# Row sums of the layer norm on GpSimd, a sort half in PSUM, and 16 instead of 14 raw rows in a two-layer graph network

## The chip, the cores and the metric

The kernel runs on one NeuronCore of a Trainium2 chip. The metric is the device time of one execution in microseconds, as the median of several runs. Stages are read from one profiled execution. Engines are named TensorE (PE), VectorE (DVE), ScalarE (ACT), GpSimd (POOL) and SyncE (SP), the last of which only issues transfers here. A "gather" is an indirect DMA that GpSimd issues: it fetches one table row for each of 128 partitions.

## The reference

12,500 nodes with 256 features, 212,500 edges sorted by destination. The node features are normalized row by row, then two graph layers follow, and the input is added at the end.

```
h = relu(layernorm(x))
h = batchnorm(h, g0, b0)
for each of two layers:
    agg = segment_sum(h[src], dst)            # 212,500 edges
    h = relu(batchnorm((h + agg) @ W1 + b1))  # 256 x 256
    h = relu(h @ W2 + b2)
out = x + h
```

The layer norm of a row needs its sum, then the sum of the squares about the mean, then one scaled and shifted pass.

## The kernel before, in words

The nodes lie in 98 blocks of 128 rows (NB), 14 chunks (NCH) of 7 blocks (CH); all of them stay in the tile `acc`. The first seven chunks are the first half of the layer norm, the others the second (LB = 7). The edges are cut into 110 rows (NR) of 1932, one on each partition. `NPOS` and the copies of the table let one gather fetch several neighbouring source rows.

**Layer norm, ScalarE.** `ln_sums` (L977) makes seven row sums of a chunk as copies with an accumulated output, a small operation (L980) turns them into minus the mean, and `ln_squares` (L988) makes the sums of squares. A chunk's sums alternate with the squares of the chunk ahead. Roots are taken for each half (L995), then the raw copies (L1020) take the transposed edge lists out of PSUM into `src_raw` and `dst_raw`, and then `normalize` (L1001) writes the blocks. SyncE stores a chunk to the table `node_rows` as soon as it is normalized (`store_rows`, L565). The small arithmetic of the layer norm (`ln_variances`, `ln_rest`) is VectorE's and stands between the operations of its sort, at places that `LN_VAR_AT` and `LN_REST_AT` give and `beside_first` counts: place n is the n-th sort operation. Before, a pass of the first sort has two operations, each on 1024 elements.

**The sorts, VectorE.** For each of the 110 rows VectorE sorts 2048 keys twice in a bitonic network of 66 passes. The first 45 passes of the first sort (`in_sbuf`, L1296 and L1298) go from `keys` to `other` and back, both in SBUF. The last 21 passes and the whole second sort (`split_steps`, L1345) hold one half of the keys in SBUF and one in PSUM, so that each operation has one input of each, in four operations of 512 elements a pass. Between the sorts, and behind the second, VectorE builds the lists of source rows, lanes and codes. They are transposed on TensorE (`transpose_lists`), placed ahead of the raw group LISTS_AT, two groups before the end, and copied by ScalarE and VectorE.

**Raw rows.** The edges of the first RAWS = 14 rows are summed without the sorted lists: 16 gathers of 128 single edges a row (L679), 224 in all, each into one of RAW_SLOTS = 11 slots. Gather k waits until TensorE is done with gather k - 11. TensorE multiplies each by a one-hot matrix from ScalarE (`hot_of_raw`, L1041, L1045) at L779. This can begin once the table is stored, and lies beside the list building. SyncE puts the strided copies of the table beside it (L600), paced by `raw_done` up to COPIES_UNTIL. The sums are kept in `early` and merged by VectorE, MERGED_AT_ONCE for each row, into `acc` in the walk.

**The walk.** Rows 14 to 109 are then walked: 8 gathers a row (L697), 34 matmul instructions (L830), and VectorE adds the sums to the blocks (L1582). The gathers land in a ring of 38 places, two rows of edges. When the two blocks of a pair are complete, TensorE transposes them (L855) and multiplies by W1a (L872, L876); `pairs_late` says after which row, at most one pair a row, and none before row RAWS + 1. Layer 2 walks all 110 rows, in part twice.

**Order.** Each engine's queue is in program order, and waits stand in it. GpSimd's queue: constants, a cast and `node_steps` (L668), a wait for the stored table, 224 raw gathers, 768 gathers of walk 1, then layer 2. TensorE's queue ahead of the raw sums: the transposes of the raw lists (L728), 32 transposes of the edge lists into all eight banks (L735), a wait for the raw copies, two lane products, 98 products of the batch norm's mean (L746).

Of the kernel before, what the change touches and what calls it, by code (L numbers as in the profile page):

```python
# [14 lines left out]
P = 128  # L15
N = 12500
D = 256
# [8 lines left out]
CH = 7  # L26
NCH = NB // CH
LB = NCH // 2
# [14 lines left out]
LR = 1932  # L43
NR = (E + LR - 1) // LR
TAIL = E - (NR - 1) * LR
SORT = 2048
# [46 lines left out]
LN_VAR_AT = (18, 54)  # L93
LN_REST_AT = (30, 62)
# [3 lines left out]
RAWS = 14  # L98
RAW_TILES = RAWS * RAW
RAW_SLOTS = 11  # L100
# [8 lines left out]
FIRST_LANES_AT = 72  # L109
MERGED_AT_ONCE = 2  # L110
# [115 lines left out]
def build(nc, x, src, dst, g0, b0, W1a, b1a, g1, bt1, W1b, b1b, W2a, b2a, g2, bt2, W2b, b2b, out):  # L226
# [4 lines left out]
    with ctx:  # L231
# [6 lines left out]
        def sem(name):  # L238
            return ctx.enter_context(nc.semaphore(name))
# [101 lines left out]
        raw_ps = tr_ps + mm_ps + [set_ps, lane_ps] + agg_ps  # L341
# [34 lines left out]
        ln_summed = sem("ln_summed")  # L376
# [48 lines left out]


# [211 lines left out]
        def _(pool):  # L638
# [31 lines left out]

            pool.wait_ge(raw_lists_ready, 1)
# [48 lines left out]
        def _(pe):  # L720
# [10 lines left out]
            for of, banks in ((src_rows, raw_ps[0:4]), (dst_rows, raw_ps[4:8])):  # L731
                for j in range(RAW):
                    if banks[j // 4] is agg_ps[0]:
                        pe.wait_ge(raw_lists_ready, 1)
                    mm = pe.transpose(banks[j // 4][:, (j % 4) * P:(j % 4 + 1) * P], of[:, j * P:(j + 1) * P], ident[:, :])  # L735
            mm.then_inc(raw_transposed, 1)

            pe.wait_ge(raw_taken, 1)
# [8 lines left out]
            mm.then_inc(bn_summed, 1)  # L747

# [55 lines left out]
            for n in range(RAW_GROUPS):  # L804
                if n == LISTS_AT:
                    transpose_lists()
                sum_raw_group(n)
                if n == 0:
                    mean_columns()
                for q in pairs_beside(n):  # L810
                    transpose_pair(q)
# [155 lines left out]
        def _(act):  # L967
# [4 lines left out]
            def ln_sums(i, k):  # L972
                act.wait_ge(x_loaded[k], i * (32 if k == LB - 1 else 16) + 16)
                act.wait_ge(ln_squared, i * LB + max(k - 1, 0))
                first = (i * LB + k) * CH
                for b in range(first, first + CH):
                    ins = act.activation(unread[b % CH], block_of(b), ACT.Copy, accum_out=ln_sum[:, b:b + 1])  # L977
                ins.then_inc(ln_summed, 1)
                act.wait_ge(ln_summed, i * LB + k + 1)
                act.activation(ln_less[:, first:first + CH], ln_sum[:, first:first + CH], ACT.Copy, scale=-1.0 / D  # L980
                               ).then_inc(ln_centred, 1)

            def ln_squares(i, k):
                act.wait_ge(ln_centred, i * LB + k + 1)
                act.wait_ge(ln_squared, i * LB + k)
                first = (i * LB + k) * CH
                for b in range(first, first + CH):
                    ins = act.activation(unread[b % CH], block_of(b), ACT.Square, bias=ln_less[:, b:b + 1],  # L988
                                         accum_out=ln_square[:, b:b + 1])
                ins.then_inc(ln_squared, 1)  # L990
# [14 lines left out]
            def ln_stats_of(i, k0, k1):  # L1005
                for k in range(k0, k1):
                    if k < LB:
                        ln_sums(i, k)
                    if k:
                        ln_squares(i, k - 1)  # L1010
# [7 lines left out]
            for to, banks in ((src_raw, raw_ps[0:4]), (dst_raw, raw_ps[4:8])):  # L1018
                for h in range(0, RAW, 4):
                    ins = act.copy(to[:, h * NR:(h + 4) * NR].rearrange("p (j g) -> p j g", g=NR), bank_tiles(banks[h // 4]))  # L1020
            ins.then_inc(raw_taken, 1)
# [6 lines left out]
            normalize(1, 0, LB)  # L1028

# [96 lines left out]
        def _(dve):  # L1126
# [134 lines left out]
            setup(dve.memset(other[:, LR:SORT], REMOVED))  # L1261
# [22 lines left out]
            step(dve.scalar_tensor_tensor(other[:, 0:LR], self_edges, REMOVED, keys[:, 0:LR], ALU.mult, ALU.add))  # L1284

            def in_sbuf(of, to, runs, beside):

                half, n = 1, 0
                while half < runs:
                    by = half  # L1290
                    while by:
                        ins, outs = [t.rearrange("p (n k) -> p n k", k=2 * by) for t in (of, to)]
                        low = ins[:, :, 0:by]
                        high = ins[:, :, 2 * by - 1:by - 1:-1] if by == half else ins[:, :, by:2 * by]
                        after()
                        step(dve.tensor_tensor(outs[:, :, 0:by], low, high, ALU.min))  # L1296
                        beside(n)
                        step(dve.tensor_tensor(outs[:, :, by:2 * by], low, high, ALU.max))  # L1298
                        beside(n + 1)
                        of, to = to, of  # L1300
                        by //= 2
                        n += 2
                    half *= 2
                return of
# [496 lines left out]
```

## Time and profile before

| | |
|---|---|
| median of 3 runs | 2776.4 us (2771.52 to 2776.82) |
| the profiled execution | 2784.43 us, span 2782.6 us |
| TensorE busy | 2371.1 us (85%) |
| GpSimd busy | 1815.2 us (65%) |
| VectorE busy | 1739.1 us (62%) |
| ScalarE busy | 551.3 us (20%) |
| first gather / first gather of walk 1 / last gather of walk 1 | 161.06 / 469.07 / 1430.84 us |

Busy shares are means over stages with different limits. GpSimd's busy time counts 0.95 us for each gather; the 0.30 us between two of them is issue and not counted. Times of stages are from the start of the span.

### The profile page before, as it was taken

Reading aid. Unit: us, or ns where it says so; the run is one execution under the profiler, and the core shown is the slowest. Engines: PE = TensorE matmul, PEld = TensorE weight load, DVE = VectorE, ACT = ScalarE, POOL = GpSimd, SP = SyncE. Lnnn points to the kernel's source line nnn. Section 1 sums busy time; section 2 is a strip of 40 time slices with the busy share of each in tenths; the row PEclk is TensorE's granted clock in tenths of the full one; section 3 lists DMA queues with packets and bytes.
Section 4 is the critical chain, followed back from the end, with each engine's and each line's share of the span. In section 5 each row is a group of like instructions: output and inputs, shape, how many; then the busy total and the mean of one; then the engine's idle time right before and its main releaser. Section 6 shows DMA issues by size and latency. Waiting matters only on the chain.

```text
span 2782.6 us, 30723 instructions
## 1 busy us (share of the span) xinstructions
PE 2371.1 (85%) x10215; PEld 1827.6 (66%) x10215; DVE 1739.1 (62%) x3502; ACT 551.3 (20%) x1605; POOL 1815.2 (65%) x1894
## 2 busy tenths in 40 slices
PE   1466777999999999999979566699999999988979
PEld 1134433878877777777758444588888888776767
DVE  7999997755555555555548577555555555544459
ACT  8975544300000000000009311000000000000038
POOL 2058777777777777777740477677777777777720
PEclk8687766999999999999989899999999999999999
DMA  9387998888888888888848999888888888888868
GB/s 309 141 261 224 285 306 254 250 260 251 253 253 255 254 255 254 254 254 254 254 153 279 328 334 325 285 283 286 287 284 284 287 285 282 260 254 253 253 203 270
DMA packets 309364, 734.28 MB, mean 264 GB/s; under 512 B 41510, under 2 KB 183730, under 8 KB 309198
## 3 DMA queue, kind: packets, MB, share of 16 engines
q0 software_dynamic: 149184, 550.97, 63.2%
q1 hardware_dynamic: 160014, 181.25, 20.8%
q8 instruction: 86, 1.41, 0.2%
q14 instruction: 80, 0.66, 0.1%
HBM read 579.47 MB, written 152.59 MB: 263 GB/s over the span
## 4 chain that ended last, share of the span: by engine, by line
PE 51%; DMA 23%; POOL 8%; SPq 8%; ACT 5%; issue 4%; DVE 1%; DVEq 0%; ACTq 0%; POOLq 0%
PE agg_ps L830 35%; DMA rows<-node_rows,src_all 17%; SPq L617 7%; PE sort_ps L955 6%; PE sort_ps L872 5%; POOL rows L697 5%; DMA rows<-node_rows,raw_list 4%; PE sort_ps L876 2%; DMA raw_more<-node_rows,raw_list 2%; PE agg_ps L779 2%; ACT acc L1001 2%; POOL raw_more L679 2%; ACT lane_code L988 1%; ACT lane_code L977 1%; POOL rows L679 1%
## 5 line engine op out<-in xcount | busy, mean ns | idle before, releaser
L697 POOL DMA_INDIRECT rows<-node_rows,src_all x1648 | 1558.2, 946 | 642.6 <-issue 346.4
L830 PE MATMUL agg_ps<-rows,work 128*128 128x256 f32 (+1 forms) x7004 | 1630.3, 387 | 188.9 <-DMA rows<-node_rows,src_all 140.8
L830 PEld LDWEIGHTS agg_ps<-rows,work 128*128 128x128 f32 x7004 | 1297.7, 191 | 494.3 <-issue 133.9
L1582 DVE SCALAR_TENSOR_TENSOR acc<-agg_ps,in_first,acc 128x256 f32 (+1 forms) x286 | 138.7, 485 | 944.1 <-PE agg_ps L830 856.7
L1032 ACT ACTIVATE bn_root<-bn_var 128x2 f32<-128x2 f32 x3 | 0.6, 203 | 1860.2 <-DVE bn_var L1168 1860.2
L679 POOL DMA_INDIRECT rows<-node_rows,raw_list x124 | 129.2, 1042 | 174.8 <-DMA node_rows<-acc 137.3
L1534 DVE TENSOR_TENSOR work<-lane_code,lane_ps 128x1024 f32<-128x1024 f32 (+1 forms) x206 | 228.1, 1107 | 1.0 <-issue 1.0
L955 PE MATMUL sort_ps<-early,work 128*128 128x256 f32 x784 | 175.3, 388 | 22.1 <-ACT work L1117 11.5
L955 PEld LDWEIGHTS sort_ps<-early,work 128*128 128x128 f32 x784 | 140.2, 194 | 57.5 <-issue 25.6
L1543 DVE TENSOR_TENSOR work<-lane_code,lane_ps 128x640 f32<-128x640 f32 x206 | 167.7, 814 | 0.0
L1117 ACT ACTIVATE work<-acc,bn_shift,bn_scale 128x128 f32<-128x128 f32 x392 | 166.5, 485 | 3.3 <-DVE bn_shift L1179 2.8
L779 PE MATMUL agg_ps<-rows,lane_code 128*128 128x257 f32 (+1 forms) x248 | 109.8, 562 | 59.6 <-DMA rows<-node_rows,raw_list 56.6
L1582 DVE SCALAR_TENSOR_TENSOR acc<-agg_ps,in_second,acc 128x256 f32 (+1 forms) x286 | 136.1, 476 | 0.0
L1524 DVE SCALAR_TENSOR_TENSOR work<-lane_ps,lane_code,work 128x128 f32<-128x128 f32 x412 | 130.5, 342 | 0.0
L679 POOL DMA_INDIRECT raw_more<-node_rows,raw_list x100 | 110.6, 1106 | 30.5 <-issue 23.5
L779 PEld LDWEIGHTS agg_ps<-rows,lane_code 128*128 128x128 f32 (+1 forms) x248 | 55.2, 260 | 106.6 <-DMA rows<-node_rows,raw_list 79.3
L1106 ACT ACTIVATE acc<-acc,self_scale 128x257 f32<-128x257 f32 (+1 forms) x196 | 79.0, 495 | 193.4 <-DMA node_rows<-acc 176.8
L1538 DVE TENSOR_TENSOR work<-lane_code,lane_ps 128x384 f32<-128x384 f32 x206 | 112.7, 547 | 0.0
L1345 DVE TENSOR_TENSOR work<-work,sort_ps 128x512 f32<-128x512 f32 x168 | 108.0, 684 | 2.9
L779 PE MATMUL agg_ps<-raw_more,lane_code 128*128 128x257 f32 x200 | 81.3, 530 | 32.2 <-DMA raw_more<-node_rows,raw_list 31.9
L872 PE MATMUL sort_ps<-early,w_a 128*128 128x256 f32 x392 | 107.2, 396 | 1.3 <-DVE early L1611 1.3
L1345 DVE TENSOR_TENSOR sort_ps<-work,sort_ps 128x512 f32<-128x512 f32 x168 | 108.2, 690 | 0.0
(246 smaller groups left out, 1844.8 us busy)
## 6 DMA issues: line engine op xcount, KB each, us to landing
node_rows<-acc SPq DMA_DIRECT2D x113, 260.0 KB, 6.3
rows<-node_rows,src_all POOLq DMA_INDIRECT x1648, 4.4
node_rows<-acc SPq DMA_DIRECT2D x27, 910.0 KB, 4.3
node_rows<-acc SPq DMA_DIRECT2D x57, 390.0 KB, 5.4
node_rows<-acc SPq DMA_DIRECT2D x28, 650.0 KB, 8.6
node_rows<-acc SPq DMA_DIRECT2D x114, 130.0 KB, 4.6
acc<-in_x SPq DMA_DIRECT2D x13, 896.0 KB, 11.0
rows<-in_x SPq DMA_DIRECT2D x13, 896.0 KB, 7.3
```

The costliest lines, as they stand in the source:

```text
L617: sp.dma_start(to, of).then_inc(group_stored[i], 16)
L679: pool.indirect_dma_start(raw_rows[k % RAW_SLOTS], None, tables[0][0:NPOS, :], bass.IndirectOffsetOnAxis(raw_src[:, j * RAWS + g:j * RAWS ...
L697: pool.indirect_dma_start(tile_rows(k, 0, ROWS_OF[t] * DP), None, tables[layer][0:NPOS if t >= LAST_STRIDED else TABLE, :], bass.IndirectO ...
L779: pe.matmul(bank[:, 0:D + 1], raw_hots[n % RAW_HOTS][0:edges, (j - first) * P:(j - first + 1) * P], raw_rows[k % RAW_SLOTS][0:edges, 0:D + ...
L830: mm = pe.matmul(bank[:, 0:width], hot[:, unit * P:(unit + 1) * P], tile_rows(k, row, width), start=(start and n == 0), stop=(stop and n = ...
L872: mm = pe.matmul(to, w_a[layer][:, k, o * P:(o + 1) * P], sum_major[:, m % 2, k, :], start=(o == 0 and k == 0), stop=(last and k == KC - 1 ...
L955: mm = pe.matmul(mm_ps[b % 2][:, 0:D], act_major[:, b % CH, k, :], w_b[layer][:, k, :], start=(k == 0), stop=(k == KC - 1))
L1117: ins = act.activation(act_major[:, b % CH, k, :], half_block(b, k), ACT.Relu, bias=bn_shift[:, k:k + 1], scale=bn_scale[:, k:k + 1])
L1345: step(dve.tensor_tensor(place, low, high, op))
L1534: dve.tensor_tensor(hot[:, 0:2 * n * P].rearrange("p (j f) -> p j f", f=2 * P), codes[:, 0:n].unsqueeze(2).to_broadcast([P, n, 2 * P]), la ...
L1543: dve.tensor_tensor(hot[:, FIRST_AT[0] * P:(FIRST_AT[0] + m) * P].rearrange("p (j f) -> p j f", f=P), lanes[:, 0:m].unsqueeze(2).to_broadc ...
L1582: dve.scalar_tensor_tensor(to, sums, lanes[:, g:g + 1], to, ALU.mult, ALU.add).then_inc(sums_added, 1)
```

## The change

GpSimd gets the row sums of chunks 3 to 6 and 9 to 12, 56 of the 98 blocks, ahead of its wait for the stored table. It folds a chunk's seven blocks of 256 by adding halves: 128, 64, 32 columns, then the two chunks of a pair together, down to one. Each add waits for the one before it. ScalarE sums the other six chunks, in a new order, and makes all squares. The first sort goes through `split_steps` from its first pass. The raw copies need only two banks at a time, in turns with TensorE, and come after the normalizing. There are 16 raw rows in 9 slots, merged three at a time. The places between the sort's operations are doubled and shifted, as a pass now has four.

```diff
+SUMMED_BY_POOL = ((3, 4), (5, 6), (9, 10), (11, 12))
-LN_VAR_AT = (18, 54)
-LN_REST_AT = (30, 62)
-RAWS = 14
+LN_VAR_AT = (38, 68)
+LN_REST_AT = (50, 76)
+RAWS = 16
-RAW_SLOTS = 11
+RAW_SLOTS = 9
-FIRST_LANES_AT = 72
-MERGED_AT_ONCE = 2
+FIRST_LANES_AT = 96
+MERGED_AT_ONCE = 3
-        raw_ps = tr_ps + mm_ps + [set_ps, lane_ps] + agg_ps
+        raw_ps = [lane_ps, agg_ps[1]]
+        RAW_LISTS = [(of, first) for of in (src_rows, dst_rows) for first in range(0, RAW, 4)]
...
+            def add_halves(to, of, width):
+                nonlocal steps
+                if steps:
+                    pool.wait_ge(pool_step, steps)
+                pool.tensor_tensor(to, of[:, :, 0:width], of[:, :, width:2 * width], ALU.add).then_inc(pool_step, 1)
+                steps += 1
+
+            for i, chunks in enumerate(SUMMED_BY_POOL):
+                for n, c in enumerate(chunks):
+                    pool.wait_ge(x_loaded[c % LB], loaded_by(c))
+                    add_halves(half_sums, chunk_of(c), P)
+                    add_halves(half_sums[:, :, 0:64], half_sums, 64)
+                    add_halves(few_sums[:, n * CH:(n + 1) * CH, :], half_sums, 32)
+                for width in (16, 8, 4, 2):
+                    add_halves(few_sums[:, :, 0:width], few_sums, width)
+                add_halves(ln_sum[:, chunks[0] * CH:(chunks[1] + 1) * CH].unsqueeze(2), few_sums, 1)
+                pool.wait_ge(pool_step, steps)
+                pool.sem_inc(pool_summed, 1)
...
+            def transpose_raw(i):
+                if i >= len(raw_ps):
+                    pe.wait_ge(raw_taken, i - len(raw_ps) + 1)
+                of, first = RAW_LISTS[i]
+                for j in range(first, first + 4):
+                    mm = pe.transpose(raw_ps[i % 2][:, (j - first) * P:(j - first + 1) * P], of[:, j * P:(j + 1) * P], ident[:, :])
+                mm.then_inc(raw_transposed, 1)
+
+            pe.wait_ge(raw_lists_ready, 1)
+            for i in range(len(raw_ps)):
+                transpose_raw(i)
...
             mm.then_inc(bn_summed, 1)
+            for i in range(len(raw_ps), len(RAW_LISTS)):
+                transpose_raw(i)
...
+            def ln_pool_sums(i):
+                nonlocal centred
+                act.wait_ge(pool_summed, i + 1)
+                centre(SUMMED_BY_POOL[i][0], 2)
+                centred += 1
+                act.wait_ge(ln_centred, centred)
...
-            ln_stats_of(0, 0, LB + 1)
-            ln_stats_of(1, 0, 2)
+            for c in (0, 1, 2):
+                ln_sums(c)
+                ln_squares(c)
+            ln_sums(7)
+            ln_sums(8)
+            for i in (0, 1):
+                ln_pool_sums(i)
+                for c in SUMMED_BY_POOL[i]:
+                    ln_squares(c)
+            ln_squares(7)
+            ln_squares(8)
             ln_root_of(0)
-            ln_stats_of(1, 2, LB + 1)
-            act.wait_ge(raw_transposed, 1)
...
+            ln_sums(13)
+            ln_squares(13)
+            for i in (2, 3):
+                ln_pool_sums(i)
+                for c in SUMMED_BY_POOL[i]:
+                    ln_squares(c)
...
             normalize(1, 0, LB)
+            for i, (of, first) in enumerate(RAW_LISTS):
+                to = src_raw if of is src_rows else dst_raw
+                act.wait_ge(raw_transposed, i + 1)
+                act.copy(to[:, first * NR:(first + 4) * NR].rearrange("p (j g) -> p j g", g=NR), bank_tiles(raw_ps[i % 2])
+                         ).then_inc(raw_taken, 1)
...
-            runs = in_sbuf(other, keys, SORT // 4, beside_first)
-            dve.wait_ge(raw_taken, 1)
-            assert runs is keys
-            split_steps(SORT // 4, keys, other, keys)
+            split_steps(1, keys, other, keys, beside_first)
+            dve.wait_ge(raw_taken, len(RAW_LISTS))
```

## Rows read from the trace of the kernel before

**Rows 1.** Windows of GpSimd: stretch and length, busy (instructions), PE clock, DMA share, GB/s.

```profile
161.00:469.00 308.00, 239.78 (x224) 0.72 0.93 266
200.00:270.00 70.00, 58.69 (x38) 0.71 0.82 235
270.00:432.00 162.00, 122.58 (x130) 0.70 1.02 292
469.00:1432.00 963.00, 726.58 (x768) 0.99 0.82 254
```

**Rows 2.** The chain of waits behind the last normalized block: start, us, what.

```profile
155.89 4.27 DMA node_rows<-acc
```

**Rows 3.** Timeline of GpSimd, the first gather: start, us, operation [idle before it].

```profile
161.06 1.17 POOL L679 DMA_INDIRECT rows<-node_rows,raw_list  x1 [137.31 <-DMA node_rows<-acc]
```

**Rows 4.** Timeline of ScalarE in the layer norm.

```profile
25.53 0.42 ACT L977 ACTIVATE lane_code<-acc 128x256 f32<-128x256 f32 x1
...
28.58 0.49 ACT L988 ACTIVATE lane_code<-acc,bn_stats 128x256 f32<-128x256 f32 x1
...
32.21 0.42 ACT L977 ACTIVATE lane_code<-acc 128x256 f32<-128x256 f32 x1
...
65.55 1.28 ACT L995 ACT_TABLE_LOAD   x1
...
104.07 1.76 ACT L1020 CAST src_raw<-sort_ps 128x440 int16<-128x440 f32 x4
...
107.39 1.12 ACT L1001 ACTIVATE acc<-acc,bn_stats 128x256 f32<-128x256 f32 x2
```

**Rows 5.** The tile acc up to 110 us, by groups: ns min/median/max, first and last start.

```profile
L977 ACT ACTIVATE lane_code<-acc x84: 398/400/419, 6.1 to 95.9; 128x256 f32<-128x256 f32 x84
...
L552 SPq DMA_DIRECT2D acc<-in_x x6: 2495/2544/2782, 20.8 to 33.9; - x6
...
DMA to landing us min/median/max: 5.3/11.0/15.3
```

**Rows 6.** Timeline of VectorE: sort passes, and the wait for the raw sums.

```profile
37.38 1.23 DVE L1296 TENSOR_TENSOR work<-work 128x1024 f32<-128x1024 f32 x1
...
39.77 1.23 DVE L1296 TENSOR_TENSOR work<-work 128x1024 f32<-128x1024 f32 x1
...
268.50 1.28 DVE L1345 TENSOR_TENSOR work<-work,sort_ps 128x512 f32<-128x512 f32 x2
...
271.03 1.29 DVE L1345 TENSOR_TENSOR work<-work,sort_ps 128x512 f32<-128x512 f32 x2
...
472.76 0.95 DVE L1508 COPY lane_code<-set_ps 128x440 f32<-128x440 f32 x1 [8.62 <-PE agg_ps L779]
```

**Rows 7.** Timeline of GpSimd and VectorE in the setup.

```profile
10.60 0.23 POOL L664 TENSOR_SCALAR part_place<-part_col 128x1 f32<-128x1 f32 x1
...
19.50 4.25 POOL L668 TENSOR_TENSOR rows<-rows 128x1932 f32<-128x1932 f32 x1
...
20.42 5.36 DVE L1244 TENSOR_TENSOR rows<-work 128x1932 f32<-128x1932 int32 x1
...
25.81 2.29 DVE L1246 SCALAR_TENSOR_TENSOR rows<-work,rows 128x2048 f32<-128x2048 int32 x1
...
35.17 2.17 DVE L1284 SCALAR_TENSOR_TENSOR work<-rows,work 128x1932 f32<-128x1932 f32 x1
```

**Rows 8.** DMA issues: KB each, median us from issue to landing.

```profile
rows<-node_rows,raw_list POOLq DMA_INDIRECT x124, 6.7
```

**Rows 9.** The chain of waits in walk 1.

```profile
551.91 7.37 PE agg_ps L830 x34
...
563.26 7.37 PE agg_ps L830 x34
...
638.76 7.37 PE agg_ps L830 x34
...
657.52 7.37 PE agg_ps L830 x34
```

More of the change, by code:

```diff
@@ L423, in build, with loaded_by @@
         out_stored = sem("out_stored")
+        def loaded_by(c):
+            return 16 if c < LB else 48 if c == NCH - 1 else 32
         def block_of(b):
@@ L669, in _ @@
             assert done == POOL_SETUP
+            half_sums = rows[:, 4 * GIVEN + P:4 * GIVEN + P + CH * P].rearrange("p (b f) -> p b f", f=P)
+            few_sums = rows[:, 4 * GIVEN + P + CH * P:4 * GIVEN + P + CH * P + 2 * CH * 32].rearrange("p (b f) -> p b f", f=32)
+            steps = 0
+            def add_halves(to, of, width):
[15 more added lines that the diff above has]
+                pool.sem_inc(pool_summed, 1)
             pool.wait_ge(raw_lists_ready, 1)
@@ L809, in _ @@
                     mean_columns()
+                    pe.wait_ge(raw_taken, len(RAW_LISTS))
                 for q in pairs_beside(n):
@@ L970, in _ @@
             act.sem_inc(sum_taken, 2)
[L972 to L980, printed above, removed]
-                               ).then_inc(ln_centred, 1)
@@ L983, in ln_squares @@
[L983 to L990, printed above, removed]
+            passes = centred = 0
@@ new lines, in ln_pass, with centre @@
+            def ln_pass(c, step, done):
+                nonlocal passes
+                if passes:
+                    act.wait_ge(ln_passed, passes)
+                for b in range(c * CH, (c + 1) * CH):
+                    ins = step(b)
+                ins.then_inc(ln_passed, 1)
+                passes += 1
+                if done is not None:
+                    act.wait_ge(ln_passed, passes)
+                    act.sem_inc(done, 1)
+            def centre(c, chunks):
+                act.activation(ln_less[:, c * CH:(c + chunks) * CH], ln_sum[:, c * CH:(c + chunks) * CH], ACT.Copy, scale=-1.0 / D
+                               ).then_inc(ln_centred, 1)
@@ new lines, in ln_sums @@
+            def ln_sums(c):
+                nonlocal centred
+                act.wait_ge(x_loaded[c % LB], loaded_by(c))
+                ln_pass(c, lambda b: act.activation(unread[b % CH], block_of(b), ACT.Copy, accum_out=ln_sum[:, b:b + 1]), None)
+                act.wait_ge(ln_passed, passes)
+                centre(c, 1)
+                centred += 1
+                act.wait_ge(ln_centred, centred)
+            def ln_pool_sums(i):
+                nonlocal centred
+                act.wait_ge(pool_summed, i + 1)
+                centre(SUMMED_BY_POOL[i][0], 2)
+                centred += 1
+                act.wait_ge(ln_centred, centred)
@@ L1260, in _ @@
             dve.wait_ge(setup_done, done)
-            setup(dve.memset(other[:, LR:SORT], REMOVED))
+            setup(dve.memset(keys[:, LR:SORT], REMOVED))
             setup(dve.tensor_scalar(row_base[:, :], first_block[:, :], float(P), None, ALU.mult))
@@ L1283, in _, with split_steps @@
             dve.wait_ge(setup_done, done)
[L1284 to L1304, printed above, removed]
+            step(dve.scalar_tensor_tensor(keys[:, 0:LR], self_edges, REMOVED, keys[:, 0:LR], ALU.mult, ALU.add))
             def halves(sbuf, i):
                 return (sbuf[:, i * SORT // 2:(i + 1) * SORT // 2], sort_ps[:, i * SORT // 2:(i + 1) * SORT // 2])
-            def split_steps(half, of, sbuf, to):
-                turn = 0
+            def split_steps(half, of, sbuf, to, beside=None):
+                turn = n = 0
                 while half < SORT:
```

27 lines of the change are left out of this document (9 added, 18 removed).

## Prediction

> **What bounds the kernel now.** I read the windows of GpSimd first, then the chain of waits and the timeline at the ends of each stage. From its first gather to the end of the first walk GpSimd never rests: 224 raw gathers in 308.0 us, then 768 walk gathers in 963 us, 1.25 us each [rows 1, 3]. In the walk that pace holds to within 3 us (768 x 1.25 = 960), so there a row of edges costs 8 gathers, 10.0 us of GpSimd. In the raw stage 224 x 1.25 = 280, so 28 us are stretch; it lies almost wholly where VectorE builds lists (38 gathers in 70 us; at 1.25 they take 47.5). Beside the second sort there is none: 130 gathers in 162 us, 1.246 each [rows 1]. Vector's chain is second: it is out of work 8.62 us before the raw sums let it go on, at 464.1 us [rows 6]. Ahead of all that stands ScalarE: the last normalized block leaves at 155.89, its store lands 4.3 us later, and the first gather, after 137.31 us of waiting for that store, goes at 161.06 [rows 2, 3]. So two quantities decide: when the table is stored, and how many gathers GpSimd has to issue after it.
>
> **Part 1: row sums on GpSimd.** For ScalarE a chunk's sum pass is 28.58 - 25.53 = 3.05 us and its square pass 32.21 - 28.58 = 3.63 [rows 4]. Eight sum passes go (24.4 us), and the raw copies, 107.39 - 104.07 = 3.3 us, move behind the normalizing. That is 27.7 us at best, but the new order waits. ScalarE starts at 6.1 [rows 5], so chunks 0 to 2, both passes, end at 6.1 + 3 x 6.7 = 26.2. Chunk 7 is next; its load is issued at 20.8, and a load takes 11.0 us in the median: 31.8, up to 36.1 with the longest [rows 5]. Sums of 7 and 8 end at 38.0.
>
> GpSimd's price: its subtraction of 1932 elements took 4.25 us, 2.2 ns an element, and its one-element operation 0.23 [rows 7]. A pair of chunks is 2 x (896 + 448 + 224) + 434 = 3570 output elements in 11 instructions: 7.85 + 11 x 0.31 (0.23 and a gap of 0.08) = 11.3 us. Starting at 23.75, when the subtraction ends, pair 0 is done at 35.1 if nothing disturbs it.
>
> It is disturbed. Vector's comparison of 1932 elements began under that subtraction, took 5.36 us, and ended 2.03 us behind GpSimd's end, about what such a comparison needs alone (2.17 for the same length): it had stood still until GpSimd was through [rows 7]. The new adds begin exactly when Vector has its setup operations with two SBUF inputs to do (2.29, 2.17 and two more of that size, [rows 7]) and the first sort pass, whose two inputs are both in SBUF still. If each waits for one add (2.0, 1.0 or 0.5 us) and each add for one of them, Vector loses 5 to 10 us and pair 0 moves to about 45. I take 7; the ends are 0 (no alternation) and 10. In the Trainium skill, GPSIMD Engine Reference, sections "Specifications" and "Key points", the shared SBUF interface is contended by Vector instructions in a two-port mode or with two SBUF inputs. By it the setup collides, as I took from the row, and a sort pass with one input in PSUM doesn't; the 130 unstretched gathers of [rows 1] agree with the second half, and if the rule failed there the adds would collide all through the sort (rival 4).
>
> ScalarE's schedule from there: squares of 3 and 4 (7.3) to 52.3; pair 1 at 45 + 11.3 = 56.3, squares to 63.6; of 7 and 8 to 70.9. The root waits for Vector's variance at place 38 of the sort, 9.5 passes of 2.53 and 1.3 of list work behind 37.38, or 62.7, plus 7: covered. Root and table load 1.5, chunk 13 6.7, four square passes 14.8: 93.9, against 104.07. Without any collision the same steps give 38.0, 45.3, 53.7, 61.0, wait to 62.7, then 85.7. Normalizing takes 155.89 - 107.39 = 48.5, store and first gather 5.2 [rows 2 to 4]. First gather: 93.9 + 53.7 = 147.6, which is **13.5 us earlier**; 21.7 without collision, 11.5 with the full 10 us.
>
> **Part 2: the sort half in PSUM.** A pass costs 39.77 - 37.38 = 2.39 in SBUF and 271.03 - 268.50 = 2.53 mixed [rows 6]; 45 passes: +6 us on Vector. With 7 of collision and some 3 of waiting at place 68 (variance of the second half, due at 83 + 7, where the squares end at 93.9) its chain ends at 464.1 + 16 = 480. It is hidden by the raw stage, whose last lists are wanted at tile 248, near 490. Cost nothing; with that cover gone, what exceeds 10 us. The raw copies behind the normalizing (3.3 us and six turns with TensorE, about 10 us) lie beside the first gathers' latency; TensorE has nothing from them for the first 10 us today either. Up to 2 us.
>
> **Part 3: 16 raw rows in 9 slots.** 32 more raw gathers: +40.0 us. 16 fewer walk gathers: -20.0. The first gathers of the walk don't wait for anything else, so this is paid in full: +20.0. The 28 us of stretch stay, since both list builds still fall into the raw stage. With 11 slots a gather may be 13.75 us old before it stops GpSimd; with 9, 11.25. It lands after 6.7 in the median [rows 8], and a matmul follows. I take 1 us, the range 0 to 5.
>
> In the walk TensorE is slower than GpSimd where a pair is finished in each row (563.26 - 551.91 = 11.35 us a row) and faster afterwards (657.52 - 638.76 = 18.8 for two) [rows 9]. Today the pairs due early end at rows 15 to 25; by the planner's formula they will end at 17 to 29, thirteen in a row, while the walk starts two light rows nearer. The lead grows 1.35 us a row, and today's 3 us over 960 show the ring already full. Three more such rows: +4 us (0 to 6). MERGED_AT_ONCE 3 gives Vector one more merge a row, under that 11.35; nothing.
>
> **Sum.** -13.5 + 40.0 - 20.0 + 1 + 4 = **+11.5 us**. The profiled execution took 2784.4 (span 2782.6), 8.0 above the median shown; it would become 2795.9, and the median 2776.4 becomes **2787.9**. What a measurement of this kernel can tell from no change is about 0.2%, 5.5 us.
>
> **Rivals.**
> 1. No collision in the setup: the add and Vector's operations overlap, the gather starts at 139.4. -21.7 + 40 - 20 + 1 + 4 = +3.3, 2780, within 0.2%. For it: I read the collision from a single overlap. Against it: the 5.36 us row. Chance 0.22.
> 2. Faster: ScalarE never waits, neither for chunk 7 nor for GpSimd or the variance. Then the full 27.7 us, and with TensorE's extra rows also absorbed, -27.7 + 20 = -7.7, 2768.7. It decides from a first gather before 135.5 (20 + 5.5 below 161.06). For it: only 3 passes and 11 squares are left at 26.2, 51 us. Against it: chunk 7 can hardly land before 31. Chance 0.12.
> 3. GpSimd's adds are dearer, on narrow pieces of 1 to 16 elements above all. If a pair takes 15 us, pair 3 is done at 24 + 10 + 60 = 94, its squares at 101.3, the first gather goes at 155: -6 + 25 = +19. At 17 us it goes at 163, no earlier than now: +2 + 25 = +27, 2803. It decides from 13.2 us a pair (34 + 4 x 13.2 + 7.3 = 93.9 again). Against it: nothing in the rows but the price per element. Chance 0.10.
> 4. The mixed passes collide with the adds too: 44 adds at half a Vector operation of 0.63 us each is 14 us more on both engines, the first gather goes at about 155, +19, 2796. Against it: the second sort beside the gathers. Chance 0.04.
> The forecast itself has 0.52; its own range is +4 to +18.
>
> **Numbers.** Slower by over 0.2%: 0.52 less a little for its lower edge, with 3 and 4: 0.64. Within: 0.24. Faster: 0.12. Range: from no collision and no stalls (-21.7 + 20 = -1.7, a little below) to the full collision with all stalls (-11.5 + 20 + 6 + 5 = +19.5) and part of rival 3: **2773 to 2800**.
>
> **What would show it.** First raw gather at 147.6 (139 or 155: rivals 1, 4); the Vector setup and first pass ending near 47 instead of 40; pairs of adds of 11.3 us; ScalarE's stops at chunk 7, at pair 0 and pair 1; 256 raw gathers in about 349 us; 752 walk gathers in 946; first walk gather near 496, last one 11 us later than now; Vector waiting for raw sums, not the reverse. I am wrong if the start is before 136, if the raw stage stretches less than 28 us, or if GpSimd stops for lists or slots.

## The result, and the profile after

The changed kernel takes **2788.4 us** (median of 5 runs, 2786.2 to 2790.3) where the kernel before takes 2775.3 (5 runs, 2771.5 to 2776.8): a ratio of 1.0049 [1.0034, 1.0064], 13 us slower. The forecast was 2787.9 and slower.

Each stage is read from its first and last gather. The kernel before stands in the table twice, since a second profiled execution of it was taken with the experiments (`before_again`). Before, the raw copies lie ahead of the normalizing and take 3.3 of the 107.4 us.

| us from the start | before | before, again | after | forecast of after |
|---|---|---|---|---|
| normalizing begins | 107.4 | 107.8 | 97.3 | 93.9 |
| first gather | 161.1 | 161.5 | 150.9 | 147.6 |
| raw stage, its length | 308.0 | 306.6 | 350.9 | 349 |
| first gather of walk 1 | 469.1 | 469.6 | 501.8 | 496 |
| walk 1, its length | 961.8 | 961.1 | 945.8 | 946 |
| last gather of walk 1 | 1430.8 | 1430.6 | 1447.6 | |
| span | 2782.6 | 2770.4 | 2785.4 | |

Windows of GpSimd in the changed kernel, as in [rows 1]:

```profile
151.00:502.00 351.00, 271.43 (x257) 0.72 0.85 246
215.00:290.00 75.00, 62.42 (x42) 0.76 0.69 197
290.00:450.00 160.00, 119.82 (x127) 0.67 0.96 280
502.00:1448.00 946.00, 711.79 (x752) 0.99 0.82 253
```

The pace is that of before: 1.25 us a gather in the walk and beside the second sort (127 in 160 us), and a visible stretch only where lists are built (42 in 75 us, which at 1.25 take 52.5). So what moved is the start, 10.2 us earlier, and the number of gathers, 32 more before the walk and 16 fewer in it. The store's landing and the first gather, from the chain of waits and the timeline of GpSimd [rows 2, 3]:

```profile
145.70 4.28 DMA node_rows<-acc
```

```profile
150.88 1.19 POOL L710 DMA_INDIRECT rows<-node_rows,raw_list  x1 [71.67 <-DMA node_rows<-acc]
```

GpSimd's 137.3 us of waiting for the store have become 71.7: the adds take 55 us of time that it had to spare (23.9 to 79.2), and the store lands 10 us earlier. Their timeline (start, us, operation):

```profile
19.67 4.25 POOL L676 TENSOR_TENSOR rows<-rows 128x1932 f32<-128x1932 f32 x1
23.88 4.00 POOL L687 TENSOR_TENSOR rows<-acc 128x896 f32<-128x896 f32 x1
27.96 4.59 POOL L687 TENSOR_TENSOR rows<-rows 128x448 f32<-128x448 f32 x2
...
36.59 7.40 POOL L687 TENSOR_TENSOR rows<-rows 128x448 f32<-128x448 f32 x6
44.07 1.01 POOL L687 TENSOR_TENSOR bn_stats<-rows 128x14 f32<-128x14 f32 x1
...
58.02 2.10 POOL L687 TENSOR_TENSOR rows<-acc 128x896 f32<-128x896 f32 x1 [0.24 <-POOL bn_stats L687]
60.21 1.88 POOL L687 TENSOR_TENSOR rows<-rows 128x448 f32<-128x448 f32 x2
...
64.40 3.81 POOL L687 TENSOR_TENSOR rows<-rows 128x448 f32<-128x448 f32 x6
```

The same add of 896 elements takes 4.00 us at 23.88 and 2.10 at 58.02; the six narrow ones 7.40 and then 3.81. VectorE, at the same time:

```profile
20.58 5.36 DVE L1308 TENSOR_TENSOR rows<-work 128x1932 f32<-128x1932 int32 x1
25.98 4.05 DVE L1310 SCALAR_TENSOR_TENSOR rows<-work,rows 128x2048 f32<-128x2048 int32 x1
...
34.49 4.04 DVE L1316 SCALAR_TENSOR_TENSOR rows<-rows 128x1932 f32<-128x1932 f32 x1
...
45.93 4.89 DVE L1389 TENSOR_TENSOR sort_ps<-work 128x512 f32<-128x512 f32 x2
50.86 1.29 DVE L1389 TENSOR_TENSOR work<-work,sort_ps 128x512 f32<-128x512 f32 x2
```

The operation that took 2.29 us in [rows 7] takes 4.05, and the second sort pass starts at 50.86 where it started at 39.77 [rows 6]. From there on the passes have one input in PSUM, and neither they (2.53 us each) nor the adds (2.10) are slowed; some small operations of VectorE between the passes still are (late_adds, below). What waited for what between 16 and 150 us (us in total, times, longest):

```profile
ACT bn_stats L1026 <- POOLq L700: 11.9, 2, 6.7
ACT lane_code L1032 <- DMA acc<-in_x: 5.6, 1, 5.6
DVE bn_stats L1252 <- ACTq L1023: 2.4, 1, 2.4
ACT bn_stats L1052 <- DVE bn_stats L1252: 1.0, 1, 1.0
```

Of the 27.7 us that ScalarE was relieved of, 18.5 went to its own waits: 5.6 for chunk 7, 11.9 for the first two pairs of sums, 1.0 for the variance. Before, it waited 3.2 us in the same stretch, for a load, so the waits have grown by 15.3. At the other end, around 500 us, VectorE's timeline shows that its lists now have time to spare:

```profile
494.20 0.17 DVE L1540 TENSOR_SCALAR_CACHE_REDUCE check_sum<-lane_ps 128x12 f32<-128x12 f32 x1 [15.07 <-PE lane_ps L825]
...
505.51 0.95 DVE L1553 COPY lane_code<-set_ps 128x440 f32<-128x440 f32 x1 [8.68 <-PE agg_ps L817]
```

The wait for the raw sums, 8.7 us, is as it was [rows 6]; the one for TensorE ahead of it has grown from 2.6 to 15.1. In walk 1 the chain of waits shows TensorE at 11.35 us a row as in [rows 9], from the first of these lines to the last in ten steps:

```profile
562.52 7.37 PE agg_ps L869 x34
573.87 7.37 PE agg_ps L869 x34
...
676.00 7.37 PE agg_ps L869 x34
```

### The profile page after: what moved, and what is told of

Its sections match the earlier page's. It is cut to its first block, busy times and chain, and to the rows that moved or that the text cites. A ratio compares the mean times of both kernels' runs of the same rounds, so it can differ in the third digit from the quotient of the medians.

```text
span 2785.4 us, 30795 instructions
## 1 busy us (share of the span) xinstructions
PE 2375.7 (85%) x10211; PEld 1826.7 (66%) x10211; DVE 1750.0 (63%) x3580; ACT 544.2 (20%) x1531; POOL 1885.3 (68%) x1954
## 4 chain that ended last, share of the span: by engine, by line
PE 49%; DMA 23%; POOL 10%; SPq 7%; issue 5%; ACT 4%; DVE 3%; DVEq 0%; ACTq 0%; POOLq 0%
PE agg_ps L869 31%; DMA rows<-node_rows,src_all 16%; POOL rows L728 7%; SPq L625 7%; PE sort_ps L994 6%; PE sort_ps L911 5%; DMA rows<-node_rows,raw_list 4%; PE agg_ps L817 3%; PE sort_ps L915 2%; DMA raw_more<-node_rows,raw_list 2%; ACT acc L1058 2%; POOL rows L710 1%; ACT acc L1170 1%; POOL raw_more L710 1%; PE sort_ps L894 1%
## 5 line engine op out<-in xcount | busy, mean ns | idle before, releaser
L869 PEld LDWEIGHTS agg_ps<-rows,work 128*128 128x128 f32 x6936 | 1282.2, 191 | 481.5 <-issue 120.0
L710 POOL DMA_INDIRECT rows<-node_rows,raw_list x172 | 183.5, 1067 | 123.8 <-DMA node_rows<-acc 71.7
L817 PE MATMUL agg_ps<-rows,lane_code 128*128 128x257 f32 (+1 forms) x344 | 139.8, 528 | 75.0 <-DMA rows<-node_rows,raw_list 72.2
L994 PE MATMUL sort_ps<-early,work 128*128 128x256 f32 x784 | 174.2, 386 | 19.6 <-ACT work L1181 11.3
L1389 DVE TENSOR_TENSOR work<-work,sort_ps 128x512 f32<-128x512 f32 x258 | 166.2, 683 | 4.3
L1389 DVE TENSOR_TENSOR sort_ps<-work,sort_ps 128x512 f32<-128x512 f32 x258 | 166.3, 688 | 0.0
L817 PEld LDWEIGHTS agg_ps<-rows,lane_code 128*128 128x128 f32 (+1 forms) x344 | 75.0, 250 | 130.7 <-DMA rows<-node_rows,raw_list 96.5
L911 PE MATMUL sort_ps<-early,w_a 128*128 128x256 f32 x392 | 107.8, 398 | 1.5 <-DVE early L1656 1.5
L817 PE MATMUL agg_ps<-raw_more,lane_code 128*128 128x257 f32 (+1 forms) x168 | 74.4, 569 | 38.0 <-DMA raw_more<-node_rows,raw_list 37.6
L710 POOL DMA_INDIRECT raw_more<-node_rows,raw_list x84 | 87.9, 1046 | 27.2 <-issue 18.3
```

What stands on the lines that cost most here:

```text
L710: pool.indirect_dma_start(raw_rows[k % RAW_SLOTS], None, tables[0][0:NPOS, :], bass.IndirectOffsetOnAxis(raw_src[:, j * RAWS + g:j * RAWS ...
L817: pe.matmul(bank[:, 0:D + 1], raw_hots[n % RAW_HOTS][0:edges, (j - first) * P:(j - first + 1) * P], raw_rows[k % RAW_SLOTS][0:edges, 0:D + ...
L869: mm = pe.matmul(bank[:, 0:width], hot[:, unit * P:(unit + 1) * P], tile_rows(k, row, width), start=(start and n == 0), stop=(stop and n = ...
L911: mm = pe.matmul(to, w_a[layer][:, k, o * P:(o + 1) * P], sum_major[:, m % 2, k, :], start=(o == 0 and k == 0), stop=(last and k == KC - 1 ...
L994: mm = pe.matmul(mm_ps[b % 2][:, 0:D], act_major[:, b % CH, k, :], w_b[layer][:, k, :], start=(k == 0), stop=(k == KC - 1))
L1389: step(dve.tensor_tensor(place, low, high, op))
```

## The experiments

All profiles are read as above. "Lists" is when VectorE has written the last list word, "gap" the idle time of GpSimd just before its first walk gather (0.3 where it doesn't wait). "Before beside it" is the median of the kernel before in the same session; sessions differ, so kernels are compared by their ratios.

| kernel | first gather | lists | gap | first walk gather | last of walk 1 | time | before beside it | ratio |
|---|---|---|---|---|---|---|---|---|
| before, again | 161.5 | 459.4 | 0.3 | 469.6 | 1430.6 | | | |
| after | 150.9 | 479.1 | 0.3 | 501.8 | 1447.6 | 2788.4 | 2775.3 | 1.0049 [1.0034, 1.0064] |
| rows_alone | 161.3 | 459.5 | 0.3 | 509.6 | 1454.9 | 2796.6 | 2774.6 | 1.0076 [1.0060, 1.0093] |
| sums_14 | 150.3 | 478.6 | 30.6 | 483.9 | 1446.6 | 2788.6 | 2774.6 | 1.0050 [1.0034, 1.0067] |
| rows_15 | 151.0 | 480.2 | 8.6 | 485.6 | 1439.0 | 2780.8 | 2774.6 | 1.0020 [1.0011, 1.0030] |
| late_adds | 154.5 | 483.3 | 0.3 | 502.2 | 1446.9 | 2788.1 | 2774.6 | 1.0052 [1.0035, 1.0069] |
| adds_sbuf | 167.1 | 491.5 | 0.3 | 520.4 | 1466.2 | 2812.1 | 2777.6 | 1.0117 [1.0100, 1.0135] |
| copies_behind | 157.7 | 458.6 | 0.3 | 467.5 | 1429.8 | 2774.3 | 2777.6 | 0.9988 [0.9979, 0.9997] |
| psum_sort | 160.0 | 466.8 | 4.2 | 472.1 | 1433.9 | 2782.8 | 2777.6 | 1.0018 [1.0009, 1.0027] |
| three_pairs | 141.4 | 469.5 | 5.7 | 475.0 | 1428.5 | 2775.3 | 2777.6 | 0.9994 [0.9985, 1.0003] |
| mixed_15 | 141.1 | 465.4 | 0.3 | 473.0 | 1425.7 | 2765.6 | 2772.2 | 0.9974 [0.9964, 0.9984] |

### rows_alone: the 16 rows without the rest

The kernel before, with the counts of the change alone.

```diff
-RAWS = 14
+RAWS = 16
-RAW_SLOTS = 11
+RAW_SLOTS = 9
-MERGED_AT_ONCE = 2
+MERGED_AT_ONCE = 3
```

> The kernel before with 16 raw rows in 9 slots, merged three at a time, and nothing else of the change. My theory (GpSimd issues a gather each 1.25 us without rest, so 32 raw gathers more and 16 walk gathers fewer cost 20 us, and the ring in the walk some 4 to 8 more): first gather unchanged at 161, first walk gather 40 to 44 us later, last gather of walk 1 at 1451 to 1459, total 2775 + 20 to 28 = 2795 to 2803. Rival (the walk is TensorE's, a row there is worth 9.4 to 11.4 us of TensorE, so two rows fewer pay for the raw gathers in part): last walk gather at most 5 to 12 us later, total 2780 to 2787.

It took 2796.6 us, ratio 1.0076. The walk begins 40.0 us later than in the second look at before (509.6 to 469.6) and ends 24.3 later. This is the 40 - 20 + 4 of the forecast: from its first to its last gather walk 1 has 751 steps, 938.8 us at 1.25, and takes 6.5 more; the 767 steps of before (958.8) took 3.0 and 2.3 more. The raw stage is 28.3 us over its 320, and was 28.0 over its 280 before with 11 slots: the 9 slots cost nothing.

### sums_14: the changed kernel with 14 rows

```diff
-RAWS = 16
+RAWS = 14
-RAW_SLOTS = 9
+RAW_SLOTS = 11
-MERGED_AT_ONCE = 3
+MERGED_AT_ONCE = 2
```

> The changed kernel with 14 raw rows in 11 slots, merged two at a time: only the row sums on GpSimd and the sort half in PSUM are left of the change. My theory: first gather at 150.9, raw gathers end at 150.9 + 309.5 = 460, but VectorE's list chain ends only at 479 (20 us later than before, by collision, mixed passes and its wait for the variance), so GpSimd waits some 20 to 25 us for the lists and the walk starts at about 485; last walk gather about 1447, total 2785 to 2792, no better than 16 rows. Rival (the two extra raw rows are the whole loss): the walk starts at 460, total 2765 to 2768, faster than before by 0.3%.

It took 2788.6, the same as after. GpSimd's timeline at the end of the raw stage:

```profile
452.36 0.94 POOL L710 DMA_INDIRECT rows<-node_rows,raw_list  x1 [0.30 <-issue]
483.85 0.94 POOL L728 DMA_INDIRECT rows<-node_rows,src_all  x1 [30.55 <-issue]
```

GpSimd is through with its raw rows at 453 and stands still for 30.6 us, because VectorE's lists, 19.2 us later than before (478.6 to 459.4), aren't there. So the two extra rows of the change are filler for a hole that its other parts make: with 14 rows the lists set the start of the walk, with 16 the gathers do, and they cost 14 and 13 us.

### rows_15: one row between the two

```diff
-RAWS = 16
+RAWS = 15
-RAW_SLOTS = 9
+RAW_SLOTS = 10
```

> The changed kernel with 15 raw rows in 10 slots. My theory: 150.9 + 300 + 31 = 482, the lists are ready at about 484, so both chains end together: walk starts at about 485, 760 gathers in 955, last walk gather 1441, total 2780 to 2784. Rival (rows cost nothing, only the table's time matters): same as the changed kernel, 2788.

2780.8 us, ratio 1.0020: the best of the three counts, some 8 us under after by the two ratios, and still not faster than before. The walk starts at 485.6, again 5.4 us behind the lists (480.2), as in sums_14 (5.2). Adding that to the lists of after gives 484.4; it starts its walk at 501.8, so 17.4 us of gathers lie behind the moment at which it could have begun.

### late_adds: the adds begin behind the first sort pass

```diff
+            pool.wait_ge(sort_step, 5)
             for i, chunks in enumerate(SUMMED_BY_POOL):
```

> The changed kernel with one wait more: GpSimd begins its adds only when VectorE is through with the first sort pass, so that the adds meet no VectorE operation with two SBUF inputs. My theory: VectorE's first pass ends at 40 to 41 instead of 50.8 and its lists about 8 us earlier; ScalarE waits longer for pair 0 (51.5 instead of 45), so the first gather goes at 151 to 155; GpSimd's count is unchanged, total 2787 to 2793. If the adds then take 11.3 us a pair or less and VectorE's mixed passes still 2.53, mixed passes don't collide. Rival (the collision costs its 10 us in the end time): total 2778 to 2781.

The collision in the setup and the first pass is gone. GpSimd's first add, and VectorE's first pass and the start of its second:

```profile
41.27 2.10 POOL L687 TENSOR_TENSOR rows<-acc 128x896 f32<-128x896 f32 x1 [17.74 <-DVE sort_ps L1390]
```

```profile
37.16 2.10 DVE L1390 TENSOR_TENSOR work<-work 128x512 f32<-128x512 f32 x2
39.19 2.01 DVE L1390 TENSOR_TENSOR sort_ps<-work 128x512 f32<-128x512 f32 x2
41.23 1.29 DVE L1390 TENSOR_TENSOR work<-work,sort_ps 128x512 f32<-128x512 f32 x2
...
45.62 2.07 DVE L1272 TENSOR_SCALAR raw_list<-raw_list 128x256 int32<-128x256 int32 x1
```

These rows also give the price of the first pass when nothing disturbs it. Both of its inputs are still in SBUF, and its four operations of 512 elements take 4.07 us (37.16 to 41.23), where the two of 1024 took 2.39. So of the 11.1 us by which the second pass is late in after, 1.7 are this pass, 0.2 a later start and only 9.2 the collision (34.25 us from VectorE's first operation to the second pass in after, 25.01 here, 23.33 before).

The second pass starts 9.6 us earlier than in after, and an add of 896 elements takes its 2.10 from the first on; the pairs are done at 51.7, 62.4, 73.1 and 83.9, 10.7 us apart. The total, 2788.1, was as expected. What I had wrong is the lists: expected 8 us earlier, they came at 483.3, 4.2 later than in after. The waits between 16 and 120 us say why:

```profile
ACT bn_stats L1027 <- POOLq L701: 16.6, 2, 13.4
DVE bn_stats L1253 <- ACTq L1024: 12.6, 2, 8.8
```

The variance is VectorE's and stands at a fixed place in its sort. It needs ScalarE's squares, which need the sums of GpSimd, which now come 6.6 us later. VectorE, ahead of time by the collision it was spared, reaches the places and waits 12.6 us instead of 2.4. Most of the time only changed its place, from operations that took longer into a wait. Another 1.6 us is the last line shown: an operation with a single input, in SBUF, that took 0.45 in after and here 2.07, since it met an add that ran from 45.47 to 47.55. The rest of the 4.2 is not placed.

### adds_sbuf: the adds beside passes with both inputs in SBUF

The changed kernel with the first 45 passes between two SBUF tiles, as they were before; the places between the operations are halved again.

```diff
-            split_steps(1, keys, other, keys, beside_first)
+            runs = in_sbuf(other, keys, SORT // 4, beside_first)
+            assert runs is keys
+            split_steps(SORT // 4, keys, other, keys)
```

> The changed kernel with the first 45 sort passes back in SBUF, both inputs of each operation there, as before the change, and the places between them halved to match. My theory (an operation with two SBUF inputs and an add on GpSimd wait for each other): a pair of adds takes 17 to 22 us instead of 11, VectorE's passes beside them up to twice 2.39, the first gather goes at 160 to 175, lists at 490 or later, total 2800 to 2815. Rival (they don't collide in the sort, and mixed passes only cost): lists 6 us earlier than with the change, first gather at 151, total 2786 to 2789.

2812.1 us, ratio 1.0117. GpSimd's second pair (against 2.10 and 3.82 in after for the same two lines):

```profile
51.95 2.87 POOL L687 TENSOR_TENSOR rows<-acc 128x896 f32<-128x896 f32 x1
54.90 9.19 POOL L687 TENSOR_TENSOR rows<-rows 128x448 f32<-128x448 f32 x6
```

Pairs are done at 45.1, 65.2, 85.4 and 105.8: 20.2 us each, where after needs 10.7. The first gather goes at 167.1, later than before the change, and the lists come at 491.5, 12.4 later than after's although 45 passes are the cheaper kind. The Trainium skill, GPSIMD Engine Reference, sections "Specifications" and "Key points", has GpSimd contend with Vector instructions that have two SBUF inputs; these two kernels, 20.2 us a pair against 10.7, agree. So it is the sort half in PSUM that lets the adds pay; without it the first gather goes 5.6 us later than in before_again (161.5).

### copies_behind: the raw copies behind the normalizing, alone

The kernel before, with the two-bank raw copies of the change in ScalarE's and TensorE's queues; its line in ScalarE's:

```diff
-            act.wait_ge(raw_transposed, 1)
-            for to, banks in ((src_raw, raw_ps[0:4]), (dst_raw, raw_ps[4:8])):
...
+            for i, (of, first) in enumerate(RAW_LISTS):
+                to = src_raw if of is src_rows else dst_raw
+                act.wait_ge(raw_transposed, i + 1)
```

> The kernel before with one part of the change: the raw copies go through two banks and lie behind the normalizing instead of ahead of it. All sums are ScalarE's, the sort half stays in SBUF, 14 raw rows. My theory: first gather 3.3 us earlier, at 157.8; the raw gathers end at 465.8, just behind the lists (464); last walk gather at 1427.5, total 3 us less than before, 2771 to 2773. Rival (the copies now delay the first raw products or the lists hold the walk): no difference.

2774.3 us, ratio 0.9988 [0.9979, 0.9997]: the first gather goes 3.8 us earlier (157.7 to 161.5), the 3.3 us of copies and a little. Of that, 2.1 us are left at the first walk gather, as the raw stage is 309.8 us long for 308.1, and 0.9 at the last. So the copies behind the normalizing have a price of 1.7 us, within the "up to 2 us" of the prediction, and give more than they cost.

### psum_sort: this, and the whole first sort half in PSUM

```diff
-LN_VAR_AT = (18, 54)
-LN_REST_AT = (30, 62)
+LN_VAR_AT = (36, 108)
+LN_REST_AT = (60, 124)
...
-            runs = in_sbuf(other, keys, SORT // 4, beside_first)
-            assert runs is keys
-            split_steps(SORT // 4, keys, other, keys)
+            split_steps(1, keys, other, keys, beside_first)
```

> As copies_behind, and the first sort half mixed between SBUF and PSUM, with no adds on GpSimd and 14 raw rows: the price of the mixed passes alone. My theory: VectorE's lists are ready 5.9 us later (459.0 to 465), so the walk starts at about 470 to 471 although the raw gathers end at 466; total 2774 to 2778, 2 to 5 us above copies_behind. Rival (mixed passes are covered here too): equal to copies_behind.

It took 2782.8, 8.6 us over copies_behind where 2 to 5 were expected. The lists come 8.2 us later (466.8 to 458.6): 44 mixed passes at 2.53 for 2.39 make 6.2, and the first pass, which takes 4.12 us here (37.45 to 41.57), makes 1.7. The first gather comes 2.3 later, by a wait of 2.2 us of ScalarE for the variance, whose place the slower passes reach later. GpSimd waits 4.2 us for the lists, and the last walk gather is 4.1 later. The other 4.5 us lie behind walk 1. There GpSimd waits 7.3 us for the table copies in layer 2, and 5.5 in copies_behind; that is 1.8. Without these waits, last gather to end takes 1341.3 us here and 1338.4 in copies_behind, both within what executions of these kernels differ by (see "The sum" below). That the cover is thin is shown: with 14 rows the lists have only some 3 us to spare ahead of the walk (458.6 + 5.3 = 463.9, first walk gather 467.5), not the 10 of my prediction.

### three_pairs: less for GpSimd, later, and 15 rows

From here on I looked for a version that beats both. Three pairs begin behind the first pass, ScalarE sums chunks 3, 4 and 13 while it would wait, and VectorE's second variance and its rest move from places 68 and 76 to 72 and 80. These were changed together, and no run separates them.

```diff
-SUMMED_BY_POOL = ((3, 4), (5, 6), (9, 10), (11, 12))
+SUMMED_BY_POOL = ((5, 6), (9, 10), (11, 12))
-RAWS = 16
+RAWS = 15
-RAW_SLOTS = 9
+RAW_SLOTS = 10
...
+            pool.wait_ge(sort_step, 5)
...
-            for c in (0, 1, 2):
+            for c in (0, 1, 2, 3, 4):
...
+            ln_sums(13)
+            for i in (0,):
```

> A version made from the readings: GpSimd sums three pairs of chunks (5 and 6, 9 and 10, 11 and 12) and begins when VectorE is through with its first sort pass; ScalarE sums 0 to 4, 7, 8 and 13 and so has work while chunk 7 and the first pair are outstanding; 15 raw rows in 10 slots; the second variance stands at place 72 and its rest at 80, so that VectorE doesn't wait for it. My theory (two chains must get shorter together: GpSimd's gathers and VectorE's lists): first gather at 139 to 141, lists ready near 467 to 470, walk starts at 471 to 475, last walk gather at 1425 to 1429 against 1430.8 before, total 2769 to 2774, 0.1 to 0.2% faster than before. Rival (only the time of the table counts, 21 us earlier than before): total 2763 or less. Rival (adds cost more than they give in any order): 2780 or more.

Every stage came as expected, to within half a microsecond: first gather 141.4, lists 469.5, walk at 475.0, last gather of walk 1 at 1428.5. ScalarE waits in all 2.6 us in the layer norm instead of 18.5:

```profile
ACT bn_stats L1027 <- POOLq L701: 1.6, 1, 1.6
ACT lane_code L1033 <- DMA acc<-in_x: 1.0, 1, 1.0
```

The table is ready 9.5 us before that of after, with less of the work on GpSimd. But the lists are still 10 us later than before, so the walk waits for them (5.7 us), and the end of walk 1 gains only 2.1 us. The time, 2775.3, can't be told from before (0.9994 [0.9985, 1.0003]); 2769 to 2774 was expected.

### mixed_15: PSUM only while GpSimd adds

three_pairs, but only the first 15 passes go through `split_steps` (`MIXED = 16`: the steps with halves of 1 to 16); the next 30 go between two SBUF tiles again. The later places are moved to match.

```diff
-            split_steps(1, keys, other, keys, beside_first)
+            split_steps(1, keys, other, keys, beside_first, MIXED)
+            runs = in_sbuf(keys, other, 2 * MIXED, SORT // 4, beside_first, 60)
+            assert runs is keys
+            split_steps(SORT // 4, keys, other, keys)
```

> As three_pairs, but only the first 15 sort passes, those that lie beside the adds, are mixed between SBUF and PSUM; the 30 passes after them are in SBUF again. My theory: lists ready 3.9 us earlier than in three_pairs (469.5 to about 465.6), the walk starts at 471 instead of 475, last walk gather at 1424 to 1425, 6 us ahead of the kernel before; 0.15 to 0.25% faster than it. Rival (the ends of both chains are no longer what counts): no difference to three_pairs.

**2765.6 us** (9 runs, 2763.9 to 2768.5), ratio 0.9974 [0.9964, 0.9984]: faster than before by 0.26%, and by the two ratios 0.75% faster than after (1.0049 / 0.9974). The last pair is done at 73.6, and the first 15 passes run until 81.1, so the adds are over before VectorE has two SBUF inputs again. GpSimd at the start of the walk:

```profile
471.80 0.95 POOL L712 DMA_INDIRECT raw_more<-node_rows,raw_list  x1 [0.30 <-PE agg_ps L819]
473.05 0.94 POOL L730 DMA_INDIRECT rows<-node_rows,src_all  x1 [0.30 <-issue]
```

No gap: lists (465.4 + 5.3 = 470.7) and gathers (473.0) arrive within 3 us of each other, both earlier than in after. The gathers set the start of the walk, 2 us behind the 471 expected, and the last gather of walk 1 goes 4.9 us ahead of that of before where 6 were expected.

### before_again: the stop in layer 2

The kernel before, unchanged.

> The kernel before, profiled once more. My theory: first gather at 161, walk 469 to 1431 as in the profile shown, but the stop of 12.6 us between the two parts of the second walk's gathers (waiting for the table's copies) will be smaller, 1 to 8 us, and the span nearer 2775: it is what sets that profiled execution above its median. Rival: the stop is the kernel's and is 12 to 13 us again.

The profiled execution shown at first was 8 us over its median. In GpSimd's timeline there:

```profile
1757.67 0.94 POOL L697 DMA_INDIRECT rows<-node_rows,src_all  x1 [0.30 <-issue]
1770.30 0.94 POOL L697 DMA_INDIRECT rows<-node_rows,src_all  x1 [11.69 <-DMA node_rows<-acc]
```

In the second look no such wait is there, and the span is 2770.4 instead of 2782.6, though the last gather of walk 1 goes at 1430.6 and 1430.8. So the 12 us of difference belong to layer 2 and to the execution, not to the kernel. That is why the change is weighed at the last gather of walk 1 and by the medians, not by the two spans.

## Why the prediction was right, point by point

**The two quantities.** Right, and the table shows it: at the last gather of walk 1 (against 1430.6) adds_sbuf, rows_alone, after, late_adds, sums_14, rows_15, psum_sort, copies_behind, three_pairs and mixed_15 stand at +36, +24, +17, +16, +16, +8, +3, -1, -2 and -5 us, and their medians against that of before beside them at +34, +22, +13, +13, +14, +6, +5, -3, -2 and -7. But with 14 or 15 rows a third quantity decides, which I had only as a cover: the lists, which must be written 5.3 us ahead of the walk.

**ScalarE's schedule.** The 5.6 us for chunk 7 came as worked out (31.8 - 26.2), pair 0 at 45.1 for 45. Pair 1 came at 57.8 instead of 56.3, since its first adds were still disturbed (2.64 us for 2.10), and the squares of 7 and 8 ended at 72.7 instead of 70.9. The table load was over at 74.1, and the root then waited 1.0 us for the variance, which I had as covered, and went at 75.1. Half a microsecond more lies in the sum and square passes behind it. Together the first gather went at 150.9 for 147.6: the gain is 10.2 us, not 13.5. Two terms were mis-sized here. "Vector loses 7" was 9.2, still within the 5 to 10 that I gave. And I counted the first pass as 2.53 us like the mixed ones, where its four operations with both inputs in SBUF take 4.07 undisturbed (late_adds), 1.7 more than the 2.39 of before. With both, and two small operations that met adds, VectorE was at place 38 at 74.2, where the undisturbed count gave 62.7.

**GpSimd's adds.** A pair takes 10.7 us undisturbed for 11.3. Rival 3 (15 us and more) falls. Rival 1 (no collision) falls by the rows of after; late_adds, where the collision in the setup is really gone, doesn't even then reach the 139.4 of that rival, since its adds begin later. Rival 4 falls by late_adds: all 44 adds beside mixed passes, 10.7 us a pair. Rival 2 asked for a first gather before 135.5; with ScalarE kept at work it could be brought to 141.

**The lists.** "+16" was +20: against the sums above, VectorE is out of work at 496.8, of which 12.5 us are the longer wait for TensorE (15.1 for 2.6), so 20.2 later than the 464.1 of before. 6.2 are 44 mixed passes, 1.7 the first pass, 9.2 the collision, 2.4 a wait for ScalarE at place 68, where I had expected 3; under 1 is not placed. It cost nothing in after, as forecast, because two rows of gathers cover it. The cover ahead of 14 rows I gave as 10 us; it is some 3 to 5.

**The rows.** +40 and -20 are shown by rows_alone. The raw stage took 350.9 us for 349, walk 1 945.8 for 946, 7.0 us over its gathers for 3.0 before. So the +4 came out, but its working doesn't: it reckons with three more dense rows at 1.35 us, while its own rows 15 to 25 and 17 to 29 are 11 and 13, and in the traces TensorE's starts of rows lie 11.3 to 11.8 us apart for 10 rows before and for 12 in after. Two more such rows make 2.7 us; the other 1.3 are not placed, and that the size was met is luck. The 1 us for slots is nothing in rows_alone, and 1.7 of the 2.9 us by which the raw stage stretches more than before can be put down to the copies (copies_behind), which the sum left out. MERGED_AT_ONCE 3 was not tried alone.

**The sum.** At the last gather of walk 1 the change costs 16.8 us: -10.2 + 40 + 2.9 - 20 + 4, where 2.9 is the longer stretch of the raw stage. The medians differ by 13.1 and the forecast said 11.5. So between 2 and 4 us come back behind walk 1: from its last gather to the end of the span it is 1337.8 in after, with a stop of 2.1 in it, and 1339.8 in before_again. The other kernels without a stop in layer 2 have 1336 to 1341, and so have those with one, the first profile of before too (1351.8 - 11.7 = 1340.1), once GpSimd's wait for the table copies is taken off. For these two executions, then, it is no more than executions differ by. But nine of the ten kernels stand better by their medians than at the last gather of walk 1, by 0.1 to 3.9 us, and why is not shown. The forecast was nearer to the time than its steps were, and that is luck: the 3.3 us lost on the first gather and the 1.9 of the raw stage were made up behind walk 1, where nothing had been forecast.

**What stays open.** The 0.1 to 3.9 us by which the medians are better than the last gathers, and what decides whether the copies of the table stop GpSimd in layer 2 for 12 us, for 5, or not at all.

## What to carry to other kernels

Work moved to an engine that only waits is free for that engine, and not for its neighbours: look at what the other engine does in the same microseconds and from which memory. Where two chains meet (here the gathers behind a store and the lists of a sort), a change that shortens one and lengthens the other needs its filler measured again in steps of one; 14, 15 and 16 rows gave 2788.6, 2780.8 and 2788.4. And before work is moved away from an engine, ask what it will do with the time: ScalarE was relieved of 27.7 us of work and waited 15.3 us more, and with one of the four pairs given back to it and put where it had waited, the table was stored 9.5 us earlier than in after.

## What the runs showed of the hardware

- Beside VectorE's sort passes between two SBUF tiles (adds_sbuf) an add on GpSimd loses about the same whatever its length: that of 896 elements 0.77 us (2.87 for 2.10), each of the six narrow ones 0.90 (9.19 for 3.82), that of 14 elements 0.85 (1.07 for 0.22). Beside the setup operations of after, which take some 2 us each alone, the one of 896 loses 1.90 (4.00 for 2.10). That reads as taking turns by whole instructions, not as a shared rate; so a chain of small adds suffers most, 11 of them growing from 10.7 to 20.2 us.
- VectorE pays as well: two operations of 512 elements with both inputs in SBUF took 4.89 us beside the adds in after, and 2.01 without them in late_adds. An operation with one input, in SBUF, can wait too: in late_adds one of 256 elements took 2.07 us beside an add, for 0.45 in after. The mixed passes kept their 2.53 us, and the adds beside them their 10.7 a pair.
- An operation of the sort on 512 elements costs 1.0 us with both inputs in SBUF (4.07 for the four of late_adds' first pass) and 0.63 with one in PSUM (2.53 for four), while two of 1024 with both in SBUF take 2.39. Why isn't shown.
- The wait of GpSimd for the table copies in layer 2 was 11.7 us in one execution of a kernel and absent in the next, while the last gather of walk 1 differed by 0.2 us.
